# A two-layer transformer block on one core: instruction orders of all engines and the choice of PSUM fill banks rewritten

## The reference

```python
for l in (0, 1):
    q, k, v = x @ Wq[l], x @ Wk[l], x @ Wv[l]      # 32 or 16 query heads, 8 key/value heads
    s = softmax(q @ k.T / sqrt(head_dim))
    x = layernorm(x + (s @ v) @ Wo[l])
    h = silu(gate(x)) * up(x)                      # 768 or 688 hidden features
    x = layernorm(x + down(h))
```

## Time and profile before

| what | value |
|---|---|
| median of 3 runs | 352.78 us (351.83 to 353.12) |
| the profiled execution | 352.02 us, span 350.2 us |
| mean granted clock of TensorE | 0.903 |
| PE busy | 296.1 us (85%) |
| DVE busy | 254.2 us (73%) |
| ACT busy | 221.5 us (63%) |
| POOL busy | 213.6 us (61%) |
| chain that ended last | PE 68%, DVE 17%, issue 4%, ACT 3% |

### The profile page before, as it was taken

One profiled execution on the slowest core, in us unless ns is written; L12 is line 12 of the kernel. 1 busy time (PEld: TensorE's weight loads), 2 busy tenths in 40 slices (PEclk: granted clock), 3 DMA queues, 4 the chain that ended last, 5 costly groups with the idle time before them and its releaser, 6 DMA issues.

```text
span 350.2 us, 7093 instructions
## 1 busy us (share of the span) xinstructions
PE 296.1 (85%) x2608; PEld 206.3 (59%) x2608; DVE 254.2 (73%) x405; ACT 221.5 (63%) x408; POOL 213.6 (61%) x297
## 2 busy tenths in 40 slices
PE   8314667765777788999999999999999999999993
PEld 7202332222344354676766676687779788789993
DVE  7478978678689899999997696667664756325354
ACT  2333566677686776787686896698566656564440
POOL 5947255555573677869689755754565332766745
PEclk9955565696698999999999999999999999999998
DMA  6443351026300204500042123023506000100001
GB/s 189 125 106 118 92 154 46 2 71 168 100 0 2 63 17 123 161 4 2 3 130 65 33 65 100 2 72 94 180 22 187 7 3 1 34 2 31 2 2 60
DMA packets 24889, 23.07 MB, mean 66 GB/s; under 512 B 3558, under 2 KB 24854, under 8 KB 24854
## 3 DMA queue, kind: packets, MB, share of 16 engines
q1 hardware_dynamic: 24854, 22.61, 22.7%
HBM read 10.47 MB, written 3.26 MB: 39 GB/s over the span
## 4 chain that ended last, share of the span: by engine, by line
PE 68%; DVE 17%; issue 4%; ACT 3%; SPq 3%; POOL 2%; DMA 2%; POOLq 0%; DVEq 0%; ACTq 0%
PE FB L1259 15%; PE PV L1202 11%; PE MM L1147 9%; PE FB L1284 7%; DVE MX L955 7%; DVE LV L1065 5%; PE SC L1176 5%; PE FB L1101 4%; PE SC L1181 4%; PE FB L1231 3%; ACT PB L855 2%; PE FB L1121 2%; PE FB L1214 2%; POOL LV L739 2%; PE FB L1126 2%
## 5 line engine op out<-in xcount | busy, mean ns | idle before, releaser
L955 DVE TENSOR_REDUCE MX<-MM 128x4 f32<-128x1024 f32 x96 | 117.1, 1220 | 41.1 <-PE MM L1147 40.5
L855 ACT ACTIVATE PB<-SC 128x1024 f32<-128x1024 f32 x96 | 98.1, 1021 | 33.7 <-PE SC L1176 23.6
L1147 PE MATMUL MM<-KS,QS 62*128 62x256 bf16 (+1 forms) x384 | 48.6, 300 | 33.4 <-DVE MX L955 23.5
L721 POOL TENSOR_TENSOR HL<-HF,HH 128x256 fp32r<-128x256 f32 (+1 forms) x48 | 36.5, 769 | 36.6 <-ACT HH L832 36.5
L739 POOL TENSOR_SCALAR LV<-LB,LD,LT 128x432 f32<-128x432 uint8 x80 | 55.1, 709 | 2.0 <-DVE LB L1051 1.9
L1202 PE MATMUL PV<-PB,VP 128*32 128x256 f32 x768 | 55.4, 417 | 0.0
L1147 PEld LDWEIGHTS MM<-KS,QS 62*128 62x128 bf16 (+1 forms) x384 | 20.4, 99 | 57.0 <-DVE MX L955 35.0
L1065 DVE COPY_PREDICATED LV<-LB,LV 128x1728 f32<-128x1728 uint8 (+2 forms) x30 | 39.7, 1323 | 5.7 <-POOL LV L739 5.3
L1259 PE MATMUL FB<-XH,W 128*128 128x256 f32 x192 | 43.0, 305 | 0.0
L1259 PE MATMUL FB<-XL,W 128*128 128x256 f32 x192 | 38.5, 282 | 0.0
L1023 DVE SCALAR_TENSOR_TENSOR AA<-TH,FB 128x256 f32<-128x256 f32 (+1 forms) x48 | 19.9, 415 | 24.6 <-ACT TH L846 17.8
(11 more groups left out here) (107 smaller groups left out, 551.9 us busy)
## 6 DMA issues: line engine op xcount, KB each, us to landing
QS<-QP SPq DMA_DIRECT2D x48, 128.0 KB, 2.4
IX<-in_idx SPq DMA_DIRECT2D x10, 216.0 KB, 3.8
dw<-LO SPq DMA_DIRECT2D x10, 216.0 KB, 2.3
W1L<-dw SPq DMA_DIRECT2D x10, 216.0 KB, 3.3
KS<-KP SPq DMA_DIRECT2D x24, 64.0 KB, 2.0
XT<-in_xt SPq DMA_DIRECT2D x4, 256.0 KB, 3.2
X<-in_x SPq DMA_DIRECT2D x4, 256.0 KB, 3.2
RAW<-in_gate SPq DMA_DIRECT2D x4, 192.0 KB, 2.7
```

The costliest lines, as they stand in the source:

```text
L721: pool.tensor_tensor(HL[0:r, i, :], HF[0:r, c % 2, :], HH[0:r, i, :].bitcast(F32), ALU.subtract).then_inc(h_parts, 1)
L855: act.activation(PB[:, quad % PB_QUADS, kt, :, :], SC[:, :, :], ACT.Exp, scale=DH[layer(j)] ** -0.5).then_inc(exp_done, 1)
L955: dve.tensor_reduce(mx, MM[:, :, :].rearrange("p (f i) s -> p f i s", f=2), axis=AX.X, op=ALU.max).then_inc(max_red, 1)
L1147: ins = pe.matmul(MM[:, 2 * f + i, :], QS[lo:lo + r, j % NST, qs + h, qt * P:(qt + 1) * P], keys(j)[lo:lo + r, j % NST, ks, :], start=True ...
```

## The change

All five lists are written anew. Every list holds the same steps as before, 540 on PE, 331 on ACT, 246 on DVE, 181 on POOL and 123 on SP, so every instruction is there as before; their order and the bank of a part of the fills are others. No code besides `ORDER` changes. The parts of the diff that matter, cut (from each list the lines in which the steps spoken of below stand):

```diff
     "PE": (
-        "q.0.0@2 q.0.1 kv.0.0@0 kv.0.1 q.1.0@2 q.1.1 kv.1.0@1 max.0.0 max.0.1 max.0.2 max.0.3 max.0.4 kv.1.1 max.0.5 "
-        "max.0.6 kv.2.0@1 kv.2.1 max.0.7 max.0.8 max.0.9 mt.0.0@0 q.2.0@2 q.2.1 max.0.10 score.0.0 max.0.11 score.0.1 "
-        "max.0.12 pv.0.0.0 max.0.13 score.0.2 q.3.0@0 score.0.3 score.0.4 pv.0.0.1 score.0.5 max.0.14 pv.0.0.2 max.0.15 "
-        "max.1.0 pv.0.0.3 kv.3.0@1 score.0.6 max.1.1 mt.0.1@2 q.3.1 max.1.2 score.0.7 max.1.3 score.0.8 max.1.4 "
-        "score.0.9 pv.0.1.0 pv.0.1.1 max.1.5 score.0.10 score.0.11 pv.0.1.2 pv.0.1.3 max.1.6 score.0.12 max.1.7 max.1.8 "
-        "score.0.13 pv.0.2.0 pv.0.2.1 pv.0.2.2 score.0.14 max.1.9 mt.1.0@2 pv.0.2.3 max.1.10 score.0.15 score.1.0 "
-        "max.1.11 pv.0.3.0 pv.0.3.1 pv.0.3.2 pv.0.3.3 turn.0.0@2 kv.3.1 score.1.1 max.1.12 score.1.2 pv.1.0.0 pv.1.0.1 "
...
-        "wo.5.0@0 max.6.7 back.5.1@2 score.6.1 gu.4.0.0@1 wo.5.1 gu.4.0.1 score.6.2 gu.4.1.0@2 gu.4.1.1 gu.4.2.0@1 "
-        "gu.4.2.1 gu.4.3.0@0 gu.4.3.1 mt.6.1@2 max.7.0 score.6.3 gu.4.4.0@2 gu.4.4.1 max.7.1 score.6.4 gu.4.5.0@1 "
...
+        "q.0.0@1 q.0.1 kv.0.0@0 kv.0.1 kv.1.0@1 q.1.0@2 q.1.1 max.0.0 kv.1.1 max.0.1 max.0.2 max.0.3 max.0.4 max.0.5 "
+        "kv.2.0@1 max.0.6 max.0.7 max.0.8 q.2.0@2 mt.0.0@0 max.0.9 q.2.1 max.0.10 q.3.0@0 score.0.0 max.0.11 max.0.12 "
+        "kv.2.1 score.0.1 max.0.13 score.0.2 score.0.3 score.0.4 max.0.14 max.0.15 pv.0.0.0 score.0.5 max.1.0 pv.0.0.1 "
+        "score.0.6 mt.0.1@2 max.1.1 pv.0.0.2 score.0.7 max.1.2 pv.0.0.3 pv.0.1.0 pv.0.1.1 max.1.3 score.0.8 score.0.9 "
+        "max.1.4 score.0.10 kv.3.0@1 max.1.5 pv.0.1.2 pv.0.1.3 q.3.1 max.1.6 score.0.11 max.1.7 pv.0.2.0 pv.0.2.1 "
+        "score.0.12 max.1.8 pv.0.2.2 mt.1.0@2 score.0.13 pv.0.2.3 max.1.9 pv.0.3.0 max.1.10 score.0.14 pv.0.3.1 "
+        "score.0.15 pv.0.3.2 score.1.0 kv.3.1 pv.0.3.3 max.1.11 score.1.1 score.1.2 max.1.12 turn.0.0@2 turn.0.1@0 "
...
+        "score.6.0 turn.5.1@2 wo.5.0@0 max.6.7 back.5.1@2 score.6.1 gu.4.0.0@1 gu.4.0.1 gu.4.1.0@2 gu.4.1.1 score.6.2 "
+        "wo.5.1 gu.4.2.0@1 mt.6.1@2 max.7.0 score.6.3 gu.4.2.1 gu.4.3.0@2 max.7.1 pv.6.0.0 pv.6.0.1 pv.6.1.0 pv.6.1.1 "
...
     "ACT": (
...
-        "score.5.7 wo.4 kv.7 mt.6.0 q.7 kmid.7 stage.5.1 back.5.0 tr.4.0 score.6.0 back.5.1 score.6.1 qmid.7 wo.5 "
...
+        "kv.7 kmid.7 q.7 stage.5.1 back.5.0 tr.4.0 score.6.0 back.5.1 qmid.7 score.6.1 gu.4.0 gu.4.1 score.6.2 mt.6.1 "
...
     "DVE": (
-        "lutbits.0 scales lut2.0 lut3.0 lut4.0 max.0.0 lutbits.1 max.0.1 q8.0 max.0.2 max.0.3 max.0.4 q8.1 max.0.5 "
-        "lut2.1 q8.2 max.0.6 lut3.1 max.0.7 lut4.1 q8.3 mt.0.0 max.0.8 q8.4 max.0.9 lutbits.2 max.0.10 q8.5 max.0.11 "
-        "max.0.12 max.0.13 q8.6 lut2.2 lut3.2 lut4.2 max.0.14 max.0.15 q8.7 max.1.0 mt.0.1 lutbits.3 max.1.1 max.1.2 "
-        "max.1.3 max.1.4 lut2.3 lut3.3 lut4.3 lutbits.4 max.1.5 q8.8 max.1.6 max.1.7 mt.1.0 q8.9 max.1.8 max.1.9 "
...
+        "lutbits.0 scales lut2.0 lut3.0 lut4.0 lutbits.1 max.0.0 q8.0 max.0.1 max.0.2 max.0.3 q8.1 max.0.4 max.0.5 "
+        "lut2.1 q8.2 max.0.6 lut3.1 lut4.1 max.0.7 q8.3 mt.0.0 max.0.8 q8.4 lutbits.2 max.0.9 max.0.10 q8.5 max.0.11 "
+        "max.0.12 max.0.13 lut2.2 lut3.2 q8.6 lut4.2 max.0.14 lutbits.3 max.0.15 mt.0.1 q8.7 max.1.0 max.1.1 max.1.2 "
+        "max.1.3 lut2.3 max.1.4 lut3.3 lut4.3 lutbits.4 max.1.5 q8.8 max.1.6 max.1.7 mt.1.0 q8.9 max.1.8 max.1.9 "
...
     "POOL": (
-        "qdif.0 kdif.0 q.0 kv.0 lut1.0.0 lut1.0.1 lut1.0.2 lut1.0.3 qdif.1 lutlow.0 q8w.0 lut1.1.0 lut1.1.1 lut1.1.2 "
-        "lut1.1.3 q8w.1 q.1 q8w.2 kdif.1 q8w.3 lutlow.1 kv.1 q8w.4 lut1.2.0 q8w.5 lut1.2.1 lut1.2.2 lut1.2.3 qdif.2 "
...
+        "qdif.0 q.0 lut1.0.0 lut1.0.1 kdif.0 lut1.0.2 lut1.0.3 kv.0 lutlow.0 q8w.0 lut1.1.0 qdif.1 lut1.1.1 q8w.1 "
+        "lut1.1.2 lut1.1.3 q8w.2 kdif.1 kv.1 q8w.3 q.1 lutlow.1 q8w.4 lut1.2.0 q8w.5 lut1.2.1 lut1.2.2 lut1.2.3 qdif.2 "
...
     "SP": (
-        "ldxt.1 load.0 ldq8.0 ldq8.1 ldix.0 ldix.1 ldxt.2 ldxt.3 kstack.0.0 qstack.0.1 kstack.0.1 qstack.0.2 kstack.0.2 "
-        "qstack.0.0 qstack.1.0 ldq8.2 ldix.2 load.1 lutlow.0 ldq8.3 ldq8.4 qstack.1.1 qstack.1.2 ldq8.5 ldix.3 ldix.4 "
...
-        "kstack.6.0 kstack.6.2 mt.5.1 reload.0 reload.1 reload.2 reload.3 reload.4 reload.5 reload.6 mt.6.0 qstack.7.0 "
-        "reload.7 kstack.7.1 reload.8 kstack.7.0 kstack.7.2 qstack.7.1 reload.9 qstack.7.2 mt.6.1 mt.7.0 mt.7.1 out.4 "
...
+        "ldq8.0 ldix.0 ldix.1 load.0 load.1 load.2 qstack.0.1 ldq8.1 ldix.2 ldix.3 ldxt.1 kstack.0.0 kstack.0.1 "
+        "qstack.0.2 qstack.0.0 kstack.0.2 ldxt.2 qstack.1.0 qstack.1.1 ldq8.2 lutlow.0 kstack.1.0 ldq8.3 ldq8.4 ldx.0 "
...
+        "kstack.7.1 qstack.7.0 reload.7 reload.8 kstack.7.2 qstack.7.1 qstack.7.2 reload.9 mt.6.1 mt.7.0 out.4 mt.7.1 "
```

## The result

The new orders take 342.9 us, median of four runs (342.08 to 345.33), against 352.95 (351.83 to 353.63) for the old ones on the same chips: ratio 0.973, 95% interval 0.967 to 0.979. The profiled execution took 342.08 us, span 340.3, mean granted clock 0.942, where it was 352.02, 350.2 and 0.903. The prediction said 350.2 us with a range down to 347.0: the direction was right, the size a quarter of the true one, and the time lies outside the range. A ratio here leaves out executions over 1.5% above the fastest of their kernel; medians and ranges are of all.

What follows compares the result with a forecast made beforehand. PE and DVE racing on the one-buffer tile MM bound the first part, with DVE setting the pace; PE was full after 139 us. Terms summed to -2.6 us, giving 350.2 us on the median, range 347.0 to 354.8.

Steps and rivals of the forecast that it cites:

- start, to max.0.2: Program start: job 1's XT, issued later, lands near 17.5 us and stack transfers are pushed back; +0.9 us (0 to +2).
- q8.1, q8.2: Early DVE steps lengthened by POOL's work beside them; one of two excesses assumed to go, -0.7 us (-1.3 to 0).
- max.0.10: DVE's 2.29 us wait behind q.2.0 and q.2.1 falls to 0.7 once they are split; -1.6 us (-2.3 to 0).
- max.1.9: DVE's 2.53 us wait there shrinks, with one pv less standing before it on PE; -0.4 us (-2.0 to 0).
- max.1.11, max.1.12: More PE work before these maxima makes PE late at 1.2 GHz, at neither at 2.4 GHz; +0.6 us (0 to +2.0).
- from 111 to 139 us: PE work before each max differs by at most a step, so no change: 0 us (-1 to +1).
- max.7.0: Its 0.75 us wait for its stack's last transfer shrinks through earlier issue, mostly used up; -0.4 us (-0.8 to +1).
- The first rival: Clock levels fall elsewhere, raising max.0.13, max.1.11 and max.1.12 costs: 352.3 us; no net change, by clock or POOL, 0.31.
- max.0.14 to max.1.1: Waits of 1.08, 0.49 and 1.39 us shrink through reordering, kv.3.0 leaving max.1.1; half counted, -1.1 us (-2.2 to 0).
- The rival with the late XT: Job 1's XT lands at 22 us, DVE idles before max.0.0: about 355.5 us; slower, including a max.7.0 transfer, 0.19.
- Nothing of the waits is real: On DVE's path, late POOL table steps before lut2 take up the maxima's gain: near 352.8 us; shares 0.31 with clock.
- The second rival: Job 1's XT late in PE's queue: start +3.0, other terms halved -0.9, sum +2.1, or +4.2 with clock's upper ends; 0.19.

Runs made afterwards that it cites:

- old_q2_split: Old order with q.2's two halves on either side of max.0.9 and lutbits.2 before that maximum, nothing else: 350.66 us, ratio 0.991.
- old_heat_late: Old order plus 31 idle identity matmuls into fill bank 2 at six places between 78 and 112 us where PE waits: 347.55 us, ratio 0.985.
- old_dve: Old lists with three DVE steps (q8.2, mt.1.1, lutbits.7) moved by one place, no other engine changed: 349.43 us, ratio 0.990.
- xt1_first: New kernel with one SP step moved: the load of job 1's input goes out first again, before the feed-forward weights: 343.75 us, ratio 0.977.
- old_to_83_sp: Old order up to about 83 us, new order after it, with SP kept in the old order up to and with mt.1.0: 355.86 us, ratio 1.011.
- old_to_83_sp_heat: old_to_83_sp plus 13 idle identity matmuls into bank 2 before score.0.10, score.0.11 and max.1.7: 353.15 us, ratio 0.998.
- new_to_78: New order on all lists up to about 78 us (PE's score.0.11, DVE's max.1.5), old order after it: 348.15 us, ratio 0.989.
- new_kv3_back: New order with the PE step kv.3.0 put back before score.0.6, as in the old order: 344.35 us, ratio 0.976.
- old_four: Old lists with q.2 split around max.0.9, kv.3.0 moved behind score.0.10, 31 late idle matmuls and old_dve's three moves: 346.36 us, ratio 0.984.

## Why the prediction was wrong, point by point

How much later (+) or earlier (-) DVE comes to each step, its change over each stretch in the two profiles, against the terms:

| stretch | predicted | measured |
|---|---|---|
| start, to max.0.2 | +0.9 | +0.45 |
| to max.0.6 (q8.1, q8.2) | -0.7 | -1.4 |
| to max.0.10 | -1.6 | -1.5 |
| to max.0.13 | +0.6 | +0.3 |
| to max.1.1 | -1.1 | -2.3 |
| to max.1.8 (max.1.4) | -0.5 | -0.4 |
| to max.1.9 | -0.4 | -2.0 |
| to max.1.13 (max.1.11, max.1.12) | +0.6 | -0.8 |
| to max.2.10 ("from 111 to 139 us") | 0 | -3.5 |
| behind it (max.7.0) | -0.4 | +1.2 |

- **What bounds the kernel: right.** The race of PE and DVE on MM set the time, PE is full behind it (busy 203.62 of the 206 us from 129 us to its last matmul), and an edit of DVE's list alone or of PE's alone in that stretch moves the end.
- **max.0.10: right**, -1.6 against a wait that fell from 2.29 to 0.96, and old_q2_split shows the wait go by the edit alone, if not that its gain stays.
- **The step that failed: I took the clock's levels from the trace of before as given for each place.** The first rival had the clock fall elsewhere, but only against the new order; that it might not fall at all behind 65 us, and that this is worth something by itself, stood nowhere. Hence -0.4 for max.1.9, where the wait fell by 2.04, +0.6 for max.1.11 and max.1.12, where it came to -0.8, and 1.2 of the 3.5 us that I put at 0 (DVE's waits there fell from 2.3 to 1.1 us, and the idle matmuls alone take the same 1.2 us off this stretch). That it is the clock is shown by old_heat_late, which changes no order and brings the wait at max.1.9 from 2.53 to 0.49 and 5.4 us in all. I had the row for it: the working of max.1.11 says that at 2.4 GHz PE comes late "at neither".
- **The second failure is of size: collisions of DVE with POOL.** I saw two (q8.1 and q8.2), took half of one case, and looked for no others. Two more stood in the trace: the amount of PE work before each `max` from 111 to 139 us was indeed nearly the same, but mt.1.1 was 1.21 us shorter and lutbits.7 0.81, most of the other 2.3 us of that stretch. In the pair of profiles DVE is busy 3.8 us less up to max.2.10 (110.5 and 106.8 us). Some of that is chance: lut4.0 takes 1.50 us in the profile of before and 0.64 in that of old_dve, where nothing near it was changed.
- **max.0.14 to max.1.1:** the mechanism was right, and I counted half for fear of the exponentials; the waits of 1.08 and 1.39 fell to nothing and 0.49.
- **Start:** XT of job 1 landed at 19.4 us, not 17.5, issued at 14.86, and DVE paid a wait of 0.76. The rival with the late XT needed 22 us to decide; xt1_first shows that this microsecond is given back anyway.
- **"Nothing of the waits is real":** false here, no later lut2 waited more than 0.24 us for POOL. In old_to_83_sp it is what happened.
- **Before max.7.0:** its wait fell from 0.75 to 0.3 us as said, but 1.2 us were given back behind max.2.10, 1.0 of it in one pause of PE before max.4.0, which the profile puts down to issue. The timelines of SP and PE show more:

```profile
176.21 3.06 SPq L551 DMA_DIRECT2D KS<-KP  x3
...
180.76 0.60 PE L1148 MATMUL MM<-KS,QS 96*128 96x256 bf16 x4 [0.98 <-issue]
```

max.4.0 is the first of its job and waits for all of its stack transfers. The new list has kstack.4.0 last of them; the third of its transfers landed at 180.67 us in the trace, and PE's weight load for max.4.0 began at 180.73. I had looked for such a wait at max.7.0 alone.
- **Sums.** The second rival's is wrong: the terms besides the start add up to -3.5, half of that is -1.75 and not -0.9, so its time would be 354.0 to 356.1 us. And the low bound was cut, at 347.0: the far ends of my own terms, with the costs at 0, come to -10.1 us, or 342.7. Faster by more than 5 us had no chance of its own. The signs that I named for being right (waits below 14 us, none above 2, max.2.10 before 136) all came, and none of them could tell 2.6 us from 10.

**What stays open.** That the clock's changes are not tied to the program's start, which one trace couldn't show, the later ones do: under the same lists up to 78 us its first half-rate stretch in the span began between 15.3 us (old_heat_late) and 17.9 us (old_to_83_sp_heat). So every reading of a level above is one of a single execution. Which step holds the clock up in the new order is not shown: new_to_78 lost it again at 81.1 and 94.8 us, new_kv3_back at 74, and no single move of the old order held it. And the four edits of old_four leave 3.5 us to the new kernel (in the profiles 1.2 us of waits and 0.9 of own time behind max.1.5, and 1.5 us before it), not tried alone. Nor were the banks, or the lists of ACT and POOL, changed by themselves. Over the new kernel's own runs time and clock went together (342.08 us at 0.942, 345.33 at 0.920).

## What to carry to other kernels

Where one engine waits for TensorE in short pauses, write beside each price both levels of the granted clock, and ask what the whole sum is if the new order never lets it fall; adding idle matmuls at the pauses, where there is a free bank, is a cheap test of it, and gave about half of this change by itself (5.4 of 10.05 us). Go through the trace for instructions of one form that differ in length: here a DVE step of 0.18 us took 1.14 beside an addition of POOL, and moving it by one place took it back. Don't add gains of single edits (-2.3, -2.0, -5.4 and -3.5 us here against 352.95, -6.6 together), and read a hybrid of two schedules only after looking for waits at its seams.

## What was not expected of the hardware

- More work on TensorE made the program faster: 31 idle matmuls, 347.55 us against 352.95.
- A higher mean clock was not a shorter time: 0.968 and 344.7 us with idle matmuls early in the new kernel, 0.942 and 342.9 without; 0.963 and 350.39 with early ones in the old kernel, 0.928 and 347.55 with late ones. The Trainium skill, TensorE: Matmul & The Clock Gate, section HAM oscillation — how this bites in real kernels, describes a clock that falls between bursts of matmuls over and over; the old kernel's trace agrees, where it fell three times between 80 and 112 us alone.
- Who starts second is held: DVE's 0.18 us became 1.14 beside POOL's addition, and POOL's 1.26 became 1.86 beside DVE's table select and, in old_dve, 1.67.
